# Decoder cross attention: two sequences per score group, both in two banks, one key folded out, and key and value jobs a whole bank wide

## The chip, the cores and the metric

The kernel runs on 1 core of one Trainium2 chip. The metric is the device time of one execution of the whole kernel in microseconds. The whole kernel is a chain of twelve blocks (attention, mixture of experts, recurrence and others) on one state x of 32 sequences x 32 tokens x 256 features; the change touches one block of them, the six-layer decoder.

## The reference, cut to what matters

Each of the 6 layers runs a masked self attention, a cross attention without a mask on 257 context keys, and a two-layer MLP, each followed by a residual sum and a layer norm. There are 16 heads of 16 features.

```
def mha(xq, xkv, W, B, mask):
    q = proj(xq, W[0], B[0]); k = proj(xkv, W[1], B[1]); v = proj(xkv, W[2], B[2])
    score = jnp.einsum('bhqd,bhkd->bhqk', q, k) / math.sqrt(DH)
    if mask is not None:
        score = jnp.where(mask[:, None] == 0, -10000.0, score)
    attn = jax.nn.softmax(score, axis=-1)
    ...
def step(x, p):
    h = mha(x, x, saw, sab, mask);   x = layer_norm(h + x, lg[0], lb[0])
    h = mha(x, enc, caw, cab, None); x = layer_norm(h + x, lg[1], lb[1])
    h = jax.nn.relu(x @ W1 + B1) @ W2 + B2; x = layer_norm(h + x, lg[2], lb[2])
```

## The kernel before, in words

All data are fp32. The 32 sequences are cut into NG = 8 tiles of GB = 4 sequences (4 x 32 tokens = 128 partitions). A position is one tile in one layer, 48 in all. `decoder_layers` is a software pipeline over 51 steps. At step s, self attention (part "sa") works on position s, the keys, values and queries of cross attention ("prep") on s-1, the cross attention itself ("ca") on s-2, and its output projection ("out") and the MLP ("dm") on s-3. Steps 3 to 47 hold all the parts.

A step has 8 units. Unit u of a step does the ca work of one of 2 feature halves (cc = u // 4) and one of 4 sequences (j = u % 4), and besides it the jobs that `UNIT_JOBS[u]` lists. A job is a group of matmuls into one of 4 ring banks, read out by VectorE ("dve") or ScalarE ("act"); each job waits until the job four before it has been read out (`RB = 4`). Jobs by name: K and V make keys and values of the context; n, q the queries; S0, S1q, S1k, S2, S3, S6, S7 are self attention (S3 scores, S2 values, S6 weights x values, S7 output projection); D0 to D3 the MLP; Y the output projection of cross attention; X the value of the last key, once a layer.

The ca work of a unit goes: `scores` (4 matmuls, each on 32 rows and 64 columns of the array, 257 keys, into banks 0 and 1), `maxima` on VectorE, two exponentials on ScalarE that also give the sums, then one unit later `transposes` (bank 2) and a copy to `pT` on ScalarE, and two units later `values` (bank 3). The 257th key (the first in memory) is not in `values`: its share is multiplied in later through `spread` and `last_v`. After the 4th sequence `reciprocals` and `own_heads` on VectorE turn sums and products into `attnT`.

Each engine runs its own list in program order, which is written out by hand: for TensorE

```
for it in range(N * U):
    if ca_unit(it):     scores(*ca_unit(it))
    if ca_unit(it - 1): transposes(*ca_unit(it - 1))
    for a in jobs_in(it): job(*a)
    if ca_unit(it - 2): values(*ca_unit(it - 2))
```

VectorE takes in each unit `maxima`, what was put off, the unit's jobs, then (by unit) `reciprocals`, `own_heads`, `own_queries` (unit 2), `self_shift` (unit 3: mask, row maximum, subtraction), `self_shares` (unit 4: sum, reciprocal, product and transpose into `sa_pT`), and last the second half of a layer norm. Job S6 waits for `sa_pT` and for the copy of S2's bank into `sa_v`.

## Time and profile before

| | us |
|---|---|
| median of 3 runs (lowest, highest) | 4612.44 (4609.56, 4612.98) |
| the profiled execution's own time | 4595.03 |
| its span from the first to the last instruction | 4593.2 |
| TensorE busy in the span | 4045.7 (88%) |
| VectorE busy | 2613.4 (57%) |
| ScalarE busy | 1853.6 (40%) |

The span is the time in which instructions run; busy times are sums over an engine's instructions. A busy share over the whole span mixes blocks with different limits; the decoder's ca units lie between about 774 and 2824 us of the span.

### The profile page before, as it was taken

What the parts mean: (1) busy time and instruction counts of PE and PEld (TensorE: products, weight loads), DVE (VectorE), ACT (ScalarE), POOL (GpSimd) and SP (SyncE); (2) the same over time, 40 slices, a digit from 0 to 9 for tenths busy, and PEclk for the clock granted to TensorE, in tenths of its full rate; (3) what the DMA queues carried; (4) which work ended last, traced back from release to release, by engine and by line L of the source; (5) the groups of instructions that cost most, each with busy time, mean ns of one, the idle gap of its engine ahead of it and who ended that gap; (6) DMA issues with size and microseconds to landing.
All of it is one profiled execution on the core that took longest, in us unless ns stands there. A gap on an engine that the chain in (4) does not pass through costs nothing. (4 is left out here: it accounts for less than half of the span.)

```text
span 4593.2 us, 105087 instructions
## 1 busy us (share of the span) xinstructions
PE 4045.7 (88%) x43842; PEld 3101.4 (68%) x43842; DVE 2613.4 (57%) x5580; ACT 1853.6 (40%) x5080; POOL 300.9 (7%) x560
## 2 busy tenths in 40 slices
PE   7988995999999999999999997779588787888867
PEld 6766884777777777777777775568345577566635
DVE  3435115777777777777777774721367654345545
ACT  1221221444444444444444443212266454255523
POOL 0000101000000000000000000010211000000000
PEclk9998997999999999999999998879799888888878
DMA  4110573011111111111111100048544300000000
GB/s 148 59 58 3 203 288 99 29 33 43 51 33 43 51 35 41 51 35 40 51 35 40 51 29 9 3 160 293 172 153 145 116 0 0 25 30 28 11 1 12
DMA packets 116921, 310.54 MB, mean 68 GB/s; under 512 B 29352, under 2 KB 75625, under 8 KB 92017
## 3 DMA queue, kind: packets, MB, share of 16 engines
q1 hardware_dynamic: 113392, 295.61, 18.8%
q0 software_dynamic: 3072, 8.39, 0.5%
q8 instruction: 342, 5.60, 0.5%
q14 instruction: 115, 0.93, 0.1%
HBM read 289.01 MB, written 14.94 MB: 66 GB/s over the span
## 5 line engine op out<-in xcount | busy, mean ns | idle before, releaser
L2490 ACT ACTIVATE layers_probs<-banks,layers_negmax 128x257 f32<-128x257 f32 x768 | 357.6, 471 | 1002.7 <-DVE layers_negmax L2369 1002.7
L2213 PE MATMUL banks<-ctx_tiles,weights_a 128*128 128x257 f32 x1536 | 397.4, 381 | 0.0
L2219 PE MATMUL banks<-weights_a,ctx_tiles 128*128 128x256 f32 x1536 | 379.4, 380 | 0.0
L2219 PEld LDWEIGHTS banks<-weights_a,ctx_tiles 128*128 128x128 f32 x1536 | 285.1, 191 | 35.4
L2369 DVE TENSOR_REDUCE layers_negmax<-banks 128x2 f32<-128x514 f32 x384 | 262.3, 683 | 71.5 <-PE banks L2274 71.5
L2213 PEld LDWEIGHTS banks<-ctx_tiles,weights_a 128*128 128x128 f32 x1536 | 270.9, 191 | 26.6 <-ACT layers_KT L2467 0.4
L2274 PE MATMUL banks<-layers_KT,layers_qblk 32*64 32x257 f32 x3072 | 256.2, 403 | 26.6 <-ACT layers_probs L2490 26.3
L2282 PEld LDWEIGHTS banks<-const,layers_probs 128*128 128x128 f32 x1536 | 162.2, 141 | 149.4 <-issue 149.3
L2282 PE MATMUL banks<-const,layers_probs 128*128 128x128 f32 x1536 | 253.6, 288 | 0.0
L2349 DVE TENSOR_TENSOR layers_V<-banks,rows_a 128x256 f32<-128x256 f32 x384 | 160.2, 418 | 138.8 <-PE banks L2219 132.9
L2495 ACT COPY layers_pT<-banks 128x512 f32<-128x512 f32 x384 | 223.5, 582 | 3.3 <-PE banks L2282 3.3
L2467 ACT ACTIVATE layers_KT<-banks,layers_ca_bk 128x257 f32<-128x257 f32 x384 | 184.2, 496 | 47.8 <-PE banks L2213 47.7
L2258 PE MATMUL banks<-layers_dm_nT,weights_b 128*128 128x128 f32 x1536 | 189.3, 277 | 0.6 <-ACT layers_dm_nT L2464 0.6
L2258 PEld LDWEIGHTS banks<-layers_dm_nT,weights_b 128*128 128x128 f32 x1536 | 184.8, 194 | 3.2 <-ACT layers_dm_nT L2464 0.9
L2263 PE MATMUL banks<-weights_b,layers_hid 128*128 128x256 f32 x768 | 173.8, 379 | 1.7 <-ACT layers_hid L2481 1.7
L2294 PEld LDWEIGHTS banks<-layers_pT,layers_V 128*32 128x32 f32 x6144 | 109.7, 109 | 87.8 <-issue 78.0
L2294 PE MATMUL banks<-layers_pT,layers_V 128*32 128x64 f32 x6144 | 163.6, 224 | 0.3 <-ACT layers_pT L2495 0.3
L2263 PEld LDWEIGHTS banks<-weights_b,layers_hid 128*128 128x128 f32 x768 | 145.7, 190 | 21.7 <-issue 2.1
L2490 ACT ACTIVATION_READ_ACCUMULATOR layers_probs<-banks,layers_negmax 128x1 f32 x768 | 150.6, 196 | 0.0
L2274 PEld LDWEIGHTS banks<-layers_KT,layers_qblk 32*64 32x64 f32 x3072 | 79.5, 130 | 96.4 <-issue 39.4
L2772 PE MATMUL banks<-weights_a,ctx_tiles 128*128 128x512 f32 x256 | 129.8, 636 | 1.0 <-DVE l2x_own L2847 0.5
L2345 DVE SCALAR_TENSOR_TENSOR weights_a<-banks,layers_sa_cols,const 128x1024 f32<-128x1024 f32 x96 | 118.4, 1274 | 7.3 <-PE banks L2206 7.3
(695 smaller groups left out, 8329.3 us busy)
## 6 DMA issues: line engine op xcount, KB each, us to landing
ctx_tiles<-in_ctx SPq DMA_DIRECT2D x65, 1028.0 KB, 5.1
weights_a<-in_L_w SPq DMA_DIRECT2D x44, 1024.0 KB, 5.4
l2x_B<-positions SPq DMA_DIRECT2D x32, 1280.0 KB, 5.9
weights_b<-in_L_w SPq DMA_DIRECT2D x32, 1024.0 KB, 6.2
weights_c<-in_L_w SPq DMA_DIRECT2D x16, 1024.0 KB, 7.1
weights_b<-in_L_xattn_w SPq DMA_DIRECT2D x12, 1024.0 KB, 7.4
l0x_key_rows<-in_ctx_rows SPq DMA_DIRECT2D x32, 256.0 KB, 2.7
ctx_tiles<-in_ctx_keys SPq DMA_DIRECT2D x32, 256.0 KB, 2.8
```

What stands on the lines that cost most here:

```text
L2213: last = mm(o[:, 0:LK], ca_wk[:, c, m * P:(m + 1) * P], E.ctx[:, tile % 2, c, j * LK:(j + 1) * LK], start=c == 0, stop=c == DC - 1)
L2219: last = mm(o[:, 0:D], E.ctx[:, tile % 2, c, first:first + P], ca_wv[:, c], start=c == 0, stop=c == DC - 1)
L2258: last = mm(o[:, i * P:(i + 1) * P], dm_w1[:, c, m * P:(m + 1) * P], dm_nT[:, c], start=c == 0, stop=c == DC - 1)
L2263: last = mm(o[:, 0:D], hid[:, m], dm_w2[:, m], start=m == 0, stop=m == FC - 1)
L2274: last = mm(ps[half, r // 2, 0:LK], qblk[rows, tile % 2, cc, j], KT[rows, tile % 2, cc, j * LK:(j + 1) * LK], start=True, stop=True)
L2282: last = tr(ps[:, TURN, (KC * t + c) * P:(KC * t + c + 1) * P], probs[:, cc, j, t, 1 + c * P:1 + (c + 1) * P], E.c("ident"))
L2294: last = mm(ps[32 * i:32 * (i + 1), PV, j * 64:(j + 1) * 64], V[:, pos % 2, KC * j + c, cc * P + 32 * i:cc * P + 32 * (i + 1)], pT[:, k % ...
L2349: last = v.tensor_tensor(V[:, tile % 2, arg], o[:, 0:D], E.rA[:, 0], ALU.add)
L2369: v.tensor_reduce(negmax[:, k % 2], ps[:, 0:2, 0:LK], AX.X, ALU.max, negate=True).then_inc(s["max_ready"], 1)
L2467: last = a(KT[:, pos % 2, m, j * LK:(j + 1) * LK], o[:, 0:LK], ACT.Identity, bias=ca_bk[:, m:m + 1])
L2490: a(probs[:, cc, j, t], ps[:, t, 0:LK], ACT.Exp, bias=negmax[:, k % 2, t:t + 1], accum_out=totals[:, cc, t, j:j + 1]).then_inc(s["exp_done ...
L2495: nc.scalar.copy(pT[:, k % 2].rearrange("p t c x -> p (t c x)"), ps[:, TURN]).then_inc(s["copied"], 1)
```

## The change

Two sequences (j and j+1) go together. In even units `scores` issues 8 matmuls for both, each 256 keys wide, and puts them side by side in banks 0 and 1; `maxima` is one reduction over 1024 elements for the pair and a small operation that takes the minimum of the negated maximum and 0; `exponentials` makes all four. `transposes` come two units after the scores instead of one, `values` of both sequences together at the end of each odd unit, and `pT` has 4 buffers instead of 2.

The last key is subtracted from the others: job XK (once a layer) projects it, ScalarE makes `less_last` = bias minus that key's value, and this is the bias with which K banks are read out. The last key's own score is then 0, its weight is exp(negmax), which ScalarE makes 8 at a time (`last_e`), and `reciprocals` adds it to the sums. A K job covers two sequences (512 columns), a V job both halves of one sequence, so a step has 4 of each instead of 8 of each, and they, S0 and S2 are moved among the units. S6 is no longer put off on VectorE, and the maxima come after what was put off. On ScalarE the copy of the transposes comes first, and in even units one job (two with XK) is read out before the exponentials.

```
     UNIT_JOBS = [
-        [k_job(0), v_job(0), k_job(1), v_job(1), ("S0", None, "act")],
-        [("S1q", None, "dve"), k_job(2), ("S1k", None, "act"), k_job(3), ("n", None, "act")],
-        [("q", None, "act"), k_job(4), ("Y", None, "dve"), ("S3", None, "dve")],
-        [k_job(5), v_job(2), k_job(6)],
-        [("D0", None, "act"), v_job(3), v_job(4), v_job(5)],
-        [("S2", None, "dve"), ("D1", 0, "act"), k_job(7), v_job(6), ("S6", None, "dve")],
-        [("D2", 1, "act"), v_job(7), ("X", None, "act")],
+        [("XK", None, "act"), ("S0", None, "act"), k_job(0), v_job(0)],
+        [("S1q", None, "dve"), k_job(1), ("S1k", None, "act"), ("n", None, "act")],
+        [("q", None, "act"), v_job(1), ("Y", None, "dve"), ("S3", None, "dve")],
+        [k_job(2), v_job(2)],
+        [("D0", None, "act"), k_job(3), ("S2", None, "dve")],
+        [("D1", 0, "act"), v_job(3), ("S6", None, "dve")],
+        [("D2", 1, "act"), ("X", None, "act")],
         [("S7", None, "dve"), ("D3", None, "dve")],
     ]
...
                     need(pe, "exp_done", 2 * k)
-                    for r in (0, 2, 1, 3):
-                        rows, half = slice(32 * r, 32 * (r + 1)), slice(64 * (r % 2), 64 * (r % 2 + 1))
-                        last = mm(ps[half, r // 2, 0:LK], qblk[rows, tile % 2, cc, j], KT[rows, tile % 2, cc, j * LK:(j + 1) * LK], start=True, stop=True)
+                    for a in range(2):
+                        for r in (0, 2, 1, 3):
+                            rows, half = slice(32 * r, 32 * (r + 1)), slice(64 * (r % 2), 64 * (r % 2 + 1))
+                            last = mm(ps[half, r // 2, a * KW:(a + 1) * KW], qblk[rows, tile % 2, cc, j + a], KT[rows, tile % 2, cc, (j + a) * KW:(j + a + 1) * KW], start=True, stop=True)
...
                 for it in range(N * U):
-                    if ca_unit(it):
+                    if it % 2 == 0 and ca_unit(it):
                         scores(*ca_unit(it))
-                    if ca_unit(it - 1):
-                        transposes(*ca_unit(it - 1))
+                    if ca_unit(it - 2):
+                        transposes(*ca_unit(it - 2))
                     for a in jobs_in(it):
                         job(*a)
-                    if ca_unit(it - 2):
-                        values(*ca_unit(it - 2))
+                    for back in (3, 2):
+                        if it % 2 and ca_unit(it - back):
+                            values(*ca_unit(it - back))
...
                 def maxima(k, pos, cc, j):
-                    dve.wait_ge(s["scores_done"], k + 1)
-                    v.tensor_reduce(negmax[:, k % 2], ps[:, 0:2, 0:LK], AX.X, ALU.max, negate=True).then_inc(s["max_ready"], 1)
+                    dve.wait_ge(s["scores_done"], k // 2 + 1)
+                    peak = negmax[:, cc, :, j:j + 2]
+                    link(v.tensor_reduce(peak, ps[:, 0:2].rearrange("p t (a x) -> p t a x", a=2), AX.X, ALU.max, negate=True))
+                    v.tensor_scalar(peak, peak, 0.0, None, ALU.min).then_inc(s["max_ready"], 1)
...
                 def reciprocals(k, pos, cc, j):
                     need(dve, "exp_done", 2 * (k + 1))
-                    link(v.reciprocal(rates[:, :, 0], totals[:, cc]))
-                    link(v.tensor_tensor(rates[:, :, 1], rates[:, :, 0], probs[:, cc, :, :, 0].rearrange("p j t -> p t j"), ALU.mult))
+                    dve.wait_ge(s["last_exp"], k // GB + 1)
+                    link(v.tensor_tensor(rates[:, :, 0], totals[:, cc], last_e[:, cc], ALU.add))
+                    link(v.reciprocal(rates[:, :, 0], rates[:, :, 0]))
+                    link(v.tensor_tensor(rates[:, :, 1], rates[:, :, 0], last_e[:, cc], ALU.mult))
...
-                    if ca_unit(it):
-                        maxima(*ca_unit(it))
                     for a in put_off:
                         take(*a)
                     put_off.clear()
+                    if it % 2 == 0 and ca_unit(it):
+                        maxima(*ca_unit(it))
                     for a in jobs_in(it):
-                        if a[3] in ("S3", "S6", "D3"):
+                        if a[3] in ("S3", "D3"):
...
                 def exponentials(k, pos, cc, j):
-                    act.wait_ge(s["max_ready"], k + 1)
-                    need(act, "transposed", k - U + 1)
+                    act.wait_ge(s["max_ready"], k // 2 + 1)
+                    need(act, "transposed", k + 1 - U + 1)
                     if j == 0:
                         need(act, "spread_ready", k // GB - 1)
-                    for t in range(2):
-                        a(probs[:, cc, j, t], ps[:, t, 0:LK], ACT.Exp, bias=negmax[:, k % 2, t:t + 1], accum_out=totals[:, cc, t, j:j + 1]).then_inc(s["exp_done"], 1)
+                    for i in (j, j + 1):
+                        for t in range(2):
+                            a(probs[:, cc, i, t], ps[:, t, i % 2 * KW:(i % 2 + 1) * KW], ACT.Exp, bias=negmax[:, cc, t, i:i + 1], accum_out=totals[:, cc, t, i:i + 1]).then_inc(s["exp_done"], 1)
+                    if j == GB - 2:
+                        a(last_e[:, cc], negmax[:, cc], ACT.Exp).then_inc(s["last_exp"], 1)
```

TensorE, units 4 and 5 of a full step before the change: `weights_c,layers_sa_nT` is S2, `layers_dm_nT` is D1, `layers_sa_pT,layers_sa_v` is S6.

```order
L2274 MATMUL banks<-layers_KT,layers_qblk 64x257 x4
L2282 MATMUL banks<-const,layers_probs 128x128 x4
L2199 MATMUL banks<-const,h_state 128x128 x2
L2219 MATMUL banks<-weights_a,ctx_tiles 128x256 x6
L2294 MATMUL banks<-layers_pT,layers_V 32x64 x8
L2274 MATMUL banks<-layers_KT,layers_qblk 64x257 x4
L2282 MATMUL banks<-const,layers_probs 128x128 x4
L2232 MATMUL banks<-weights_c,layers_sa_nT 128x256 x2
L2258 MATMUL banks<-layers_dm_nT,weights_b 128x128 x8
L2213 MATMUL banks<-ctx_tiles,weights_a 128x257 x2
L2219 MATMUL banks<-weights_a,ctx_tiles 128x256 x2
L2246 MATMUL banks<-layers_sa_pT,layers_sa_v 32x64 x32
```

The same units on TensorE after the change (L2284 scores, L2292 transposes, L2241 S2, L2267 D1, L2223 V, L2255 S6, L2304 values).

```order
L2284 MATMUL banks<-layers_KT,layers_qblk 64x256 x8
L2292 MATMUL banks<-const,layers_probs 128x128 x4
L2201 MATMUL banks<-const,h_state 128x128 x2
L2216 MATMUL banks<-ctx_tiles,weights_a 128x512 x2
L2241 MATMUL banks<-weights_c,layers_sa_nT 128x256 x2
L2292 MATMUL banks<-const,layers_probs 128x128 x4
L2267 MATMUL banks<-layers_dm_nT,weights_b 128x128 x8
L2223 MATMUL banks<-weights_a,ctx_tiles 128x256 x4
L2255 MATMUL banks<-layers_sa_pT,layers_sa_v 32x64 x32
L2304 MATMUL banks<-layers_pT,layers_V 32x64 x16
```

S2 has moved to the end of unit 4, ahead of unit 5's transposes; scores stand only in unit 4, values only at unit 5's end.

VectorE at the same place before the change, from the row maxima of self attention to the copy of S2's bank.

```order
L2404 TENSOR_REDUCE layers_sa_max<-layers_sa_sc 128x16
L2405 TENSOR_TENSOR layers_sa_sc<-layers_sa_sc,layers_sa_max 128x512
L2369 TENSOR_REDUCE layers_negmax<-banks 128x2
L2349 TENSOR_TENSOR layers_V<-banks,rows_a 128x256 x3
L2373 RECIPROCAL layers_rates<-layers_totals 128x2x4
L2374 TENSOR_TENSOR layers_rates<-layers_rates,layers_probs 128x2x4
L2375 TENSOR_TENSOR layers_spread<-const,layers_rates 128x512
L2409 TENSOR_REDUCE layers_sa_sum<-layers_sa_sc 128x16
L2410 RECIPROCAL layers_sa_sum<-layers_sa_sum 128x16
L2411 TENSOR_TENSOR layers_sa_sc<-layers_sa_sc,layers_sa_sum 128x512
L2412 STREAM_TRANSPOSE layers_sa_pT<-layers_sa_sc 128x512
```

And after the change, with the copy of S2's bank (L2362) among them.

```order
L2420 TENSOR_TENSOR layers_sa_sc<-layers_sa_sc,layers_sa_max 128x512
L2381 TENSOR_REDUCE layers_negmax<-banks 128x2x2
L2382 TENSOR_SCALAR layers_negmax<-layers_negmax 128x2x2
L2362 TENSOR_TENSOR layers_sa_v<-banks,const 128x1024
L2387 TENSOR_TENSOR layers_rates<-layers_totals,layers_last_e 128x2x4
L2388 RECIPROCAL layers_rates<-layers_rates 128x2x4
L2389 TENSOR_TENSOR layers_rates<-layers_rates,layers_last_e 128x2x4
L2390 TENSOR_TENSOR layers_spread<-const,layers_rates 128x512
L2424 TENSOR_REDUCE layers_sa_sum<-layers_sa_sc 128x16
L2425 RECIPROCAL layers_sa_sum<-layers_sa_sum 128x16
L2426 TENSOR_TENSOR layers_sa_sc<-layers_sa_sc,layers_sa_sum 128x512
L2427 STREAM_TRANSPOSE layers_sa_pT<-layers_sa_sc 128x512
```

The copy of S2's bank now stands ahead of the reciprocals and of the shares of self attention; before it came after them, behind one more reduction.

## Rows read from the trace of the kernel before

**Rows 1.** Windows of one step: busy us of each engine, clock, DMA.

```profile
1500.00:1543.00 43.00, 42.11 (x476) 32.40 (x475) 31.47 (x71) 19.79 (x64) 2.47 (x6) 1.00 0.31 107
```

**Rows 2.** Waits, 900 to 2700 us: engine, line, releaser: us, times, longest.

```profile
PEld banks L2199 <- DVE weights_a L2345: 38.3, 42, 0.9
```

**Rows 3.** TensorE timeline: start us, us, line, tiles [idle before <-releaser].

```profile
1502.25 0.66 PE L2274 MATMUL banks<-layers_KT,layers_qblk 32*64 32x257 f32 x8
1502.84 0.66 PE L2282 MATMUL banks<-const,layers_probs 128*128 128x128 f32 x4
1503.34 1.03 PE L2213 MATMUL banks<-ctx_tiles,weights_a 128*128 128x257 f32 x4
1504.20 1.03 PE L2219 MATMUL banks<-weights_a,ctx_tiles 128*128 128x256 f32 x4
...
1507.11 0.43 PE L2294 MATMUL banks<-layers_pT,layers_V 128*32 128x64 f32 x16
1507.47 0.66 PE L2274 MATMUL banks<-layers_KT,layers_qblk 32*64 32x257 f32 x8
...
1512.75 0.44 PE L2199 MATMUL banks<-const,h_state 128*128 128x128 f32 x2 [0.51 <-DVE weights_a L2345]
...
1517.71 1.07 PE L2238 MATMUL banks<-weights_a,layers_sa_k 128*32 128x256 f32 x16
1518.60 0.41 PE L2294 MATMUL banks<-layers_pT,layers_V 128*32 128x64 f32 x16
...
1523.53 0.66 PE L2274 MATMUL banks<-layers_KT,layers_qblk 32*64 32x257 f32 x8 [0.38 <-ACT layers_probs L2490]
...
1529.83 1.95 PE L2258 MATMUL banks<-layers_dm_nT,weights_b 128*128 128x128 f32 x16
1531.62 1.03 PE L2213 MATMUL banks<-ctx_tiles,weights_a 128*128 128x257 f32 x4
1532.49 1.03 PE L2219 MATMUL banks<-weights_a,ctx_tiles 128*128 128x256 f32 x4
1533.44 1.10 PE L2246 MATMUL banks<-layers_sa_pT,layers_sa_v 128*32 128x64 f32 x64
1534.36 0.41 PE L2294 MATMUL banks<-layers_pT,layers_V 128*32 128x64 f32 x16
1534.58 0.61 PE L2299 MATMUL banks<-layers_spread,const 128*32 128x256 f32 x8
```

**Rows 4.** VectorE timeline of the filling steps.

```profile
799.64 0.19 DVE L2373 RECIPROCAL layers_rates<-layers_totals 128x8 f32<-128x8 f32 x1
...
802.40 0.71 DVE L2412 STREAM_TRANSPOSE layers_sa_pT<-layers_sa_sc 128x512 f32<-128x512 f32 x1
...
803.62 1.21 DVE L2351 TENSOR_TENSOR layers_sa_v<-banks,const 128x1024 f32<-128x1024 f32 x1
```

**Rows 5.** VectorE timeline of a full step.

```profile
1523.28 0.77 DVE L2403 COPY_PREDICATED_SCALAR layers_sa_sc<-mask_zero,layers_floor 128x512 f32 x1
...
1525.41 0.69 DVE L2369 TENSOR_REDUCE layers_negmax<-banks 128x2 f32<-128x514 f32 x1
```

**Rows 6.** Groups by line, 900 to 2700 us: count, busy us, mean ns.

```profile
L2369 DVE TENSOR_REDUCE layers_negmax<-banks 128x2 f32<-128x514 f32 x335 | 228.7, 683 | 50.0 <-PE banks L2274 50.0
...
L2481 ACT ACTIVATE layers_hid<-banks,layers_dm_cols 128x128 f32<-128x128 f32 x332 | 96.3, 390 | 0.0
```

**Rows 7.** TensorE timeline of the filling steps.

```profile
780.19 0.44 PE L2199 MATMUL banks<-const,h_state 128*128 128x128 f32 x2 [1.75 <-ACT layers_KT L2467]
...
804.93 1.10 PE L2246 MATMUL banks<-layers_sa_pT,layers_sa_v 128*32 128x64 f32 x64 [1.53 <-DVE layers_sa_v L2351]
```

**Rows 8.** Windows of the filling steps, with the granted clock (PEclk).

```profile
781.00:784.00 3.00, 3.00 (x18) 2.65 (x14) 0.69 (x1) 1.54 (x6) 0.00 (x0) 0.50 0.00 0
...
800.00:805.00 5.00, 3.47 (x25) 2.69 (x25) 4.86 (x9) 1.27 (x5) 0.00 (x0) 1.00 0.00 0
```

**Rows 9.** TensorE timeline of the last steps.

```profile
2795.61 1.13 PE L2274 MATMUL banks<-layers_KT,layers_qblk 32*64 32x257 f32 x8 [2.81 <-ACT layers_probs L2490]
```

More of the change, by code:

```diff
@@ L2042, in decoder_layers @@
     VC = GB * KC
+    KW = KC * P
     U = DC * GB
@@ L2046, in k_job @@
     def k_job(i):
-        return ("K", (i // GB, i % GB), "act")
+        return ("K", (i // 2, i % 2), "act")
     def v_job(i):
@@ L2106, in decoder_layers @@
                     pos = parts[PART[kind]]
-                    if pos is not None and (kind != "X" or pos % NG == 0):
+                    if pos is not None and (kind not in ("X", "XK") or pos % NG == 0):
                         at[pos, kind, arg] = len(jobs)
@@ L2157, in _ @@
                         if step >= 2:
-                            need_job(sp, step - 2, "V", VC - 1)
+                            need_job(sp, step - 2, "V", GB - 1)
                         sp.dma_start(E.ctx[:, step % 2], A["ctx"][step % NG]).then_inc(s[f"ctx{step % 2}"], 16)
@@ L2171, in _ @@
                         send(layer, "w_ca_q")
-                        need_evacuated(sp, step - 1, "K", (DC - 1, GB - 1))
+                        need_evacuated(sp, step - 1, "K", (DC - 1, 1))
                         send(layer, "w_ca_k")
-                        need_evacuated(sp, step - 1, "V", VC - 1)
+                        need_evacuated(sp, step - 1, "V", GB - 1)
                         send(layer, "w_ca_v")
@@ L2212, in job @@
                         for c in range(DC):
-                            last = mm(o[:, 0:LK], ca_wk[:, c, m * P:(m + 1) * P], E.ctx[:, tile % 2, c, j * LK:(j + 1) * LK], start=c == 0, stop=c == DC - 1)
+                            keys = E.ctx[:, tile % 2, c].rearrange("p (j k) -> p j k", j=GB)[:, 2 * i:2 * i + 2, 1:LK]
+                            last = mm(o.rearrange("p (j k) -> p j k", j=2), ca_wk[:, c, m * P:(m + 1) * P], keys, start=c == 0, stop=c == DC - 1)
                     elif kind == "V":
-                        first = arg // KC * LK + 1 + arg % KC * P
                         if arg == 0:
                             need_weights(pe, "w_ca_v", pos)
-                        for c in range(DC):
-                            last = mm(o[:, 0:D], E.ctx[:, tile % 2, c, first:first + P], ca_wv[:, c], start=c == 0, stop=c == DC - 1)
+                        for b in range(KC):
+                            first = arg * LK + 1 + b * P
+                            for c in range(DC):
+                                last = mm(o[:, b * D:(b + 1) * D], E.ctx[:, tile % 2, c, first:first + P], ca_wv[:, c], start=c == 0, stop=c == DC - 1)
+                    elif kind == "XK":
+                        need_weights(pe, "w_ca_k", pos)
+                        for m in range(DC):
+                            for c in range(DC):
+                                last = mm(o[:, m * NB:(m + 1) * NB], ca_wk[:, c, m * P:(m + 1) * P], E.last[:, c], start=c == 0, stop=c == DC - 1)
                     elif kind == "X":
@@ L2290, in values @@
                         if cc == 0:
[L2291 removed]
+                            need_evacuated(pe, pos, "V", GB - 1)
                     for c in range(KC):
                         for i in range(4):
[L2294 removed]
+                            last = mm(ps[32 * i:32 * (i + 1), PV, j * 64:(j + 1) * 64], V[:, pos % 2, KC * j + c, cc * P + 32 * i:cc * P + 32 * (i + 1)], pT[:, k % 4, i // 2, c, 64 * (i % 2):64 * (i % 2 + 1)], start=c == 0, stop=c == KC - 1)
                     last.then_inc(s["pv_done"], 1)
@@ L2465, in take @@
                     elif kind == "K":
-                        m, j = arg
-                        last = a(KT[:, pos % 2, m, j * LK:(j + 1) * LK], o[:, 0:LK], ACT.Identity, bias=ca_bk[:, m:m + 1])
+                        m, i = arg
+                        for j in (2 * i, 2 * i + 1):
+                            seq = pos % NG * GB + j
+                            last = a(KT[:, pos % 2, m, j * KW:(j + 1) * KW], o[:, j % 2 * KW:(j % 2 + 1) * KW], ACT.Identity, bias=less_last[:, pos // NG % 2, m, seq:seq + 1])
+                    elif kind == "XK":
+                        for m in range(DC):
+                            a(last_k[:, m], o[:, m * NB:(m + 1) * NB], ACT.Identity, bias=ca_bk[:, m:m + 1]).then_inc(s["last_keys"], 1)
+                        act.wait_ge(s["last_keys"], DC * (pos // NG + 1))
+                        for m in range(DC):
+                            last = a(less_last[:, pos // NG % 2, m], last_k[:, m], ACT.Identity, scale=-1.0, bias=ca_bk[:, m:m + 1])
+                        last.then_inc(s["evac_act"], 1)
+                        need_evacuated(act, pos, "XK")
+                        return
                     elif kind == "q":
```

37 lines of the change are left out of this document (20 added, 17 removed).

## The prediction

> **What bounds the kernel now.** I first read the windows. In one 43 us stretch of the decoder TensorE is busy 42.11 us, VectorE 31.47, ScalarE 19.79, at full clock [rows 1]. Busy rows of matmuls overlap, so the share alone proves little; the waits say more. In 1800 us there is one TensorE wait of note that ends on VectorE, and it comes 42 times [rows 2]: a step lasts 1800 / 42 = 42.9 us, and there are 45 full steps. Then I read TensorE's timeline of a step [rows 3] by the distance from one group's start to the next group's start, since that, and not the duration, is what a group costs. Two places in a step show a wait: 0.51 us before job n at 1512.75 (its ring bank is the one of S1q, which VectorE reads out late; the weight loads waited 0.91 by [rows 2]) and 0.38 us before the scores at 1523.53 (exponentials of the unit before). Everything else is issue. So the decoder is bound by what TensorE issues; a saving there counts in full, and a new wait there counts in full too.
>
> **What the change takes off TensorE.** Prices by start-to-start [rows 3]: scores of one unit 0.59 (1502.25 to 1502.84), transposes 0.50, a K job 0.86, values 0.36 (1507.11 to 1507.47), but only 0.22 (1534.36 to 1534.58) where a group of the same shape of tiles stands on each side. A V job costs 0.95 (1532.49 to 1533.44) instead of some 0.86 where such a tiled group follows: entering costs about 0.1. Per pair of units before: twice (0.10 entry + 0.36 + 0.59 + 0.50) = 3.10 us. After, the pair has one entry 0.10, values 0.36 + 0.22, scores 0.59 plus a second set of four, transposes 0.50 once behind scores, and once behind an ordinary job, where I put 0.42 (an estimate: 0.50 less the cost of leaving the tiled scores, for which the 0.1 of entering is the nearest number).
>
> The trace of before has no second set of scores on the same rows of the array, so it is bounded. From below: pure streaming, one 257-column matmul, half a K job = 0.43, since the four run side by side. S3 shows two sets of four 256-column matmuls in 0.89 (1517.71 to 1518.60), which is 0.43 each and nothing over. From above: the whole 0.59 again. I take 0.43, as S3 is the nearest row. Then a pair costs 0.10 + 0.58 + 1.02 + 0.92 = 2.62, that is 0.48 less. One pair of the four stood behind S3, a tiled group already, and had no entry to lose: about 0.3. Sum: 3 x 0.48 + 0.3 = 1.74 us a step.
>
> The Trainium skill (TensorE: Matmul & The Clock Gate, Part 3, what overlaps and what doesn't) says that a weight load overlaps matmuls in flight only where the row group differs. The second set of scores uses the same four row groups again, so by that sentence its loads would wait for the first set and the second set would cost 0.59 or more, and the sum would lose 0.64 us a step. S3's two sets above speak against it, though S3 loads all 128 rows; no row here shows the case itself.
>
> K and V jobs: the same matmul columns in fewer, wider banks. K goes from 257 to 256 columns: 16 columns a step, 0.03 us. XK is four 32-column products once in eight steps: nothing. VectorE: 8 reductions of 683 ns [rows 6] become 4 over 1024 elements; a 1024-element operation took 1.21 [rows 4], so 4 x (1.21 + about 0.2 for the small one), 0.2 more in all; V reads lose 4 fixed parts, about 1 us less. ScalarE gets two small exponentials. All this lies under TensorE and costs nothing by itself; the cover is TensorE's 43 us against 31.5 and 20.
>
> **The old waits.** Job n's bank is now that of V0, read long before; S1q is now waited for by q (four jobs on), some 1.9 us later. Scores wait for exponentials issued two units back. Both waits go: the idle shown is 0.51 + 0.38 for matmuls and, with the weight loads' 0.91, more; I take 1.1.
>
> **The new wait.** S2 is moved to unit 4's end, and VectorE copies its bank before reciprocals and shares. From S2's last issue: 0.20 until the reader starts, copy 1.13 (start to next start, within the 1.21 of [rows 4]), reciprocals and shares of self attention in one go, 799.64 to 802.40 + 0.71 = 3.47 us for seven operations [rows 4], one added small operation 0.2, and 0.1 to TensorE: 5.1 us. TensorE meanwhile has transposes 0.42, D1 1.79 (1529.83 to 1531.62), V3 1.73 + 0.10 = 4.04 us before S6. So S6 waits 1.1 us in each step where before it did not. Behind it on TensorE stand values, shares and the next scores: all shift. Is VectorE free when S2 ends? V2 closes unit 3's jobs; from its last issue VectorE needs 0.2 + 0.6 (V2) + 2.13 (the self shift, 1523.28 to 1525.41 [rows 5]) + 1.4 (reduction) = 4.3 us, and TensorE needs values 0.68, scores 1.02, transposes 0.50, D0 0.21 (half of 0.42: two transposes), K 1.72, S2 0.86 = 5.0. There is 0.7 us to spare, plus the 0.2.
>
> D3 is a smaller one: D2's four reads take 4 x 0.39 less what they overlap, about 1.2 [rows 6], start 0.2 after D2, and TensorE has only transposes 0.42 to 0.50 and S7 0.87 in between (V7 stood there before). I charge 0.1.
>
> **The sum.** Per full step 1.74 + 0.03 + 1.1 - 1.1 - 0.1 = 1.7 us; 45 steps: 76 us. At the ends: the last two steps have no self attention, so no S6 wait, and now show waits of one round trip (scores, maxima, exponentials) per unit, up to 2.81 us [rows 9]; a trip per pair is fewer of them. I take 8 us there and -2 for the first steps, where D1 is missing and S6 waits longer. Total 82 us. The profiled execution took 4595.03 us with a span of 4593.2, 17 below the median 4612.44; its span would fall to about 4511, and the median by the same 82 to 4530.
>
> **Rivals.**
>
> A. The second sets overlap nothing: second scores 0.59, second values 0.36. A pair then saves 0.18 instead of 0.48, a step 0.6 + 1.1 - 1.2 = 0.5; 45 x 0.5 + 5 = 28: 4584. For it: the unknown is real. Against: S3. Chance 0.12.
>
> B. The gain is eaten by waits I have not seen. ScalarE now holds four exponentials (2 x 0.9 us) in front of K reads and copies that ring banks depend on, and VectorE a 1.4 us block. If such a wait takes 0.5 to 1 us a step: 4552 to 4575. For it: the margins above are 0.1 to 0.9 us. Chance 0.20.
>
> C. Slower: the S6 wait makes the clock fall. In the filling steps S6 once waited 1.53 us and the window around it kept the clock at 1.00, that is 2.4 GHz; after a wait of 1.75 us before job n the clock stood at 0.50, 1.2 GHz, for a 3 us window [rows 7, 8]: 3 us at half speed lose 1.5 us of work. It needs a wait 0.6 longer than mine, which VectorE gives if it reaches S2 late by more than its 0.9 of slack plus 0.6, for example if the 1024-element reduction runs at twice the time per element of [rows 6] and another read delays it. A step then gives 1.7 - 0.6 - 1.5 = -0.4, and the 8 us at the end hold: 4612 + 18 - 8 = 4622, up to 4650 if the fall lasts longer. It decides from a wait of about 1.7 us. Chance 0.08.
>
> D. Nothing: the savings on TensorE exist but waits in sum stay as large as 1.7 us more: 4603 to 4622. Chance 0.06.
>
> My own case, 4500 to 4550, has 0.54.
>
> **How the numbers follow.** The predicted time is my case's, 4530. Bounds: second scores as cheap as 0.35 and the wait at 0.9 with both old waits at their longer reading give 2.2 a step, 4505; the other side reaches through B and most of A to 4588. Outside lie C, D and the far end of A, 2 in 10 at most. The profile and the runs shown differ by 17 us, but the runs among themselves by 3.4; a difference of about 0.2% (9 us) can be told. Faster: my case, A, B, 0.85; within 0.2%: 0.06; slower: 0.09.
>
> **What would show it.** In the profile after: scores as one group of 16 rows with 1.0 us to the transposes (1.2 would be A); the two values groups 0.58 together; a TensorE wait before S6 (L2255) that ends on VectorE's transpose into sa_pT, about 1.1 us, once a step; no wait on weights_a (S1q) before job n, none on exponentials; steps of about 41.2 us; clock 1.00 throughout. A new releaser once a step elsewhere means B; a clock below 1.00 in the steady windows means C. The prediction is wrong if VectorE's order costs more than the one wait counted here.

## The result, and the profile after

| | before | after |
|---|---|---|
| median (lowest, highest) | 4611.0 (4605.97, 4612.98) | 4554.01 (4547.84, 4561.3) |
| span of the profiled execution | 4593.2 | 4547.8 |
| TensorE busy | 4045.7 | 3983.5 |

The ratio is 0.9879, 95% interval [0.9859, 0.9898]: 57 us off, where 82 were forecast (4530), inside the range of 4505 to 4588.

The windows view of the changed kernel for one step answers to [rows 1]. Columns: window, its length, busy us (and instructions) of TensorE, its weight loads, VectorE, ScalarE, GpSimd, then granted clock, DMA share, GB/s.

```profile
1505.79:1547.34 41.55, 40.48 (x463) 29.73 (x459) 31.53 (x69) 20.13 (x66) 2.48 (x6) 1.00 0.31 110
1200.00:2400.00 1200.00, 1167.78 (x13166) 858.86 (x13165) 904.56 (x1951) 582.48 (x1914) 71.74 (x174) 1.00 0.13 41
```

The step is 41.55 us long (1505.79 is a first scores group, 1547.34 the same group one step on) and TensorE is idle in 1.07 of them. The waits of 900 to 2700 us, as in [rows 2]:

```profile
PE banks L2255 <- DVE layers_sa_pT L2427: 45.6, 43, 1.2
```

The wait on `weights_a` that stood in [rows 2] has gone, and the one new entry of TensorE's that ends on VectorE is the S6 wait, 43 times, 45.6 us. Now TensorE's timeline of that step, which answers to [rows 3]:

```profile
1504.78 0.65 PE L2304 MATMUL banks<-layers_pT,layers_V 128*32 128x64 f32 x32
1505.25 0.61 PE L2309 MATMUL banks<-layers_spread,const 128*32 128x256 f32 x8
1505.79 1.09 PE L2284 MATMUL banks<-layers_KT,layers_qblk 32*64 32x256 f32 x16
1506.82 0.66 PE L2292 MATMUL banks<-const,layers_probs 128*128 128x128 f32 x4
...
1510.89 1.07 PE L2247 MATMUL banks<-weights_a,layers_sa_k 128*32 128x256 f32 x16
1511.89 0.66 PE L2292 MATMUL banks<-const,layers_probs 128*128 128x128 f32 x4
...
1515.92 0.66 PE L2304 MATMUL banks<-layers_pT,layers_V 128*32 128x64 f32 x32
1516.51 1.09 PE L2284 MATMUL banks<-layers_KT,layers_qblk 32*64 32x256 f32 x16
...
1520.82 0.60 PE L2292 MATMUL banks<-const,layers_probs 128*128 128x128 f32 x4
1521.26 1.95 PE L2267 MATMUL banks<-layers_dm_nT,weights_b 128*128 128x128 f32 x16
1523.05 1.89 PE L2223 MATMUL banks<-weights_a,ctx_tiles 128*128 128x256 f32 x8
1525.99 1.10 PE L2255 MATMUL banks<-layers_sa_pT,layers_sa_v 128*32 128x64 f32 x64 [1.05 <-DVE layers_sa_pT L2427]
...
1531.20 0.60 PE L2292 MATMUL banks<-const,layers_probs 128*128 128x128 f32 x4
1531.63 1.03 PE L2260 MATMUL banks<-weights_c,layers_sa_attnT 128*128 128x256 f32 x4
1532.68 1.53 PE L2272 MATMUL banks<-weights_b,layers_hid 128*128 128x256 f32 x6
```

Read from start to start: the scores of two sequences (x16 by the trace's count, x8 before; it counts each fp32 matmul of the program twice) 1.03 (1505.79 to 1506.82; one set was 0.59 before), values of two sequences 0.59, or 0.47 in front of the shares (1504.78 to 1505.25), transposes 0.49 behind scores and 0.44 behind an ordinary job (1520.82 to 1521.26). From V3 at 1523.05 to S6 at 1525.99 are 2.94 us: a V job is 1.73, the entry 0.10, so the wait is 1.11. S7 to D3 is 1.05 (1531.63 to 1532.68), where S7 took 0.87 before.

VectorE's timeline shows what S6 waits for:

```profile
1521.02 1.22 DVE L2362 TENSOR_TENSOR layers_sa_v<-banks,const 128x1024 f32<-128x1024 f32 x1 [0.83 <-PE banks L2241]
1522.16 0.16 DVE L2387 TENSOR_TENSOR layers_rates<-layers_totals,layers_last_e 128x8 f32<-128x8 f32 x1
...
1522.79 0.69 DVE L2390 TENSOR_TENSOR layers_spread<-const,layers_rates 128x512 f32<-128x512 f32 x1
1523.40 0.68 DVE L2424 TENSOR_REDUCE layers_sa_sum<-layers_sa_sc 128x16 f32<-128x512 f32 x1
...
1525.13 0.71 DVE L2427 STREAM_TRANSPOSE layers_sa_pT<-layers_sa_sc 128x512 f32<-128x512 f32 x1
```

VectorE had been idle for 0.83 us when S2's bank came. From there the copy, the reciprocals, the spread and the shares follow without a gap, to the end of the transpose at 1525.84: 4.82 us.

**Where the time went, step by step.** The 45 full steps (3 to 47) took 1937.08 us before and 1881.40 after: 55.7 off. They are not alike: 32 steps gained 1.39 (42.94 to 41.55), the five before a layer's first step 1.28, the five first steps of layers 0.77 (43.75 to 42.98), the first full one 0.35, and two gained 0.90 and lost 0.38. In that last one the profile shows 1.51 us of TensorE idle ahead of D2's matmuls, and gives no releaser; what it was stays open, but it isn't chance: the same two steps are longer in the run with another order of the scores, below (42.01 and 43.22 there, 42.04 and 43.32 here). The steps before and behind these 45 gained another 6.0 in sum, up to the decoder's last output projection. The decoder's 61.7 and the span's 45.4 differ mostly by blocks whose code did not change, which took longer in this one execution (9.1 us before the decoder, 7.7 behind it).

Job XK answers for the layer steps; TensorE's timeline in one:

```profile
1077.94 0.98 PE L2228 MATMUL banks<-last_keys,weights_a 128*128 128x32 f32 x8
1078.76 0.42 PE L2201 MATMUL banks<-const,h_state 128*128 128x128 f32 x2
```

Four products of only 32 columns (eight matmuls by the trace's count) hold TensorE for 0.82 us (1077.94 to 1078.76), once per layer. The trace of before had this price: job X has the same four products, and to the values behind it are 0.91, of which 0.10 is the entry into the tiled group:

```profile
1107.88 0.97 PE L2223 MATMUL banks<-last_keys,weights_a 128*128 128x32 f32 x8
1108.79 0.43 PE L2294 MATMUL banks<-layers_pT,layers_V 128*32 128x64 f32 x16
```

In the same steps X now stands behind D2 and covers D3's reads: S7 to D3 is 0.86 there (1114.41 to 1115.27). An ordinary step's 1.39 less 0.82, with D3's 0.26 back, gives 0.83; measured is 0.77.

### The profile page after: what moved, and what is told of

Read it like the earlier page. It is cut to its first block and busy times, and to the rows that moved or that the text cites. A ratio compares the mean times of both kernels' runs of the same rounds, so it can differ in the third digit from the quotient of the medians.

```text
span 4547.8 us, 103588 instructions
## 1 busy us (share of the span) xinstructions
PE 3983.5 (88%) x43122; PEld 2985.0 (66%) x43122; DVE 2617.2 (58%) x5484; ACT 1875.0 (41%) x5200; POOL 300.4 (7%) x560
## 5 line engine op out<-in xcount | busy, mean ns | idle before, releaser
L2223 PE MATMUL banks<-weights_a,ctx_tiles 128*128 128x256 f32 x1536 | 363.6, 380 | 0.0
L2216 PE MATMUL banks<-ctx_tiles,weights_a 128*128 128x512 f32 x768 | 363.2, 595 | 0.0
L2517 ACT ACTIVATE layers_probs<-banks,layers_negmax 128x256 f32<-128x256 f32 x768 | 354.2, 480 | 13.5 <-DVE layers_negmax L2382 6.5
L2223 PEld LDWEIGHTS banks<-weights_a,ctx_tiles 128*128 128x128 f32 x1536 | 285.2, 191 | 76.3 <-issue 46.5
L2360 DVE TENSOR_TENSOR layers_V<-banks,rows_a 128x512 f32<-128x512 f32 x192 | 130.8, 681 | 215.5 <-PE banks L2223 215.5
L2292 PE MATMUL banks<-const,layers_probs 128*128 128x128 f32 x1536 | 244.1, 281 | 3.4 <-ACT layers_pT L2524 2.8
L2292 PEld LDWEIGHTS banks<-const,layers_probs 128*128 128x128 f32 x1536 | 171.2, 141 | 107.1 <-issue 97.1
L2381 DVE TENSOR_REDUCE layers_negmax<-banks 128x4 f32<-128x1024 f32 x192 | 233.7, 1217 | 2.8 <-PE banks L2284 2.6
L2484 ACT ACTIVATE layers_KT<-banks,layers_less_last 128x256 f32<-128x256 f32 x384 | 162.1, 480 | 157.1 <-PE banks L2216 157.1
L2284 PE MATMUL banks<-layers_KT,layers_qblk 32*64 32x256 f32 x3072 | 211.3, 389 | 0.0
L2267 PE MATMUL banks<-layers_dm_nT,weights_b 128*128 128x128 f32 x1536 | 190.4, 278 | 3.8 <-issue 3.2
L2216 PEld LDWEIGHTS banks<-ctx_tiles,weights_a 128*128 128x128 f32 x768 | 131.7, 191 | 92.8 <-issue 92.7
L2267 PEld LDWEIGHTS banks<-layers_dm_nT,weights_b 128*128 128x128 f32 x1536 | 181.8, 194 | 4.5 <-issue 3.6
L2284 PEld LDWEIGHTS banks<-layers_KT,layers_qblk 32*64 32x64 f32 x3072 | 98.5, 132 | 74.0 <-issue 41.0
L2507 ACT ACTIVATE layers_hid<-banks,layers_dm_cols 128x128 f32<-128x128 f32 x384 | 110.5, 379 | 65.9 <-PE banks L2267 65.8
L2304 PE MATMUL banks<-layers_pT,layers_V 128*32 128x64 f32 x6144 | 127.2, 222 | 4.7 <-ACT layers_pT L2524 4.7
L2304 PEld LDWEIGHTS banks<-layers_pT,layers_V 128*32 128x32 f32 x6144 | 97.8, 110 | 45.5 <-issue 40.0
```

The source lines that it names most:

```text
L2216: last = mm(o.rearrange("p (j k) -> p j k", j=2), ca_wk[:, c, m * P:(m + 1) * P], keys, start=c == 0, stop=c == DC - 1)
L2223: last = mm(o[:, b * D:(b + 1) * D], E.ctx[:, tile % 2, c, first:first + P], ca_wv[:, c], start=c == 0, stop=c == DC - 1)
L2267: last = mm(o[:, i * P:(i + 1) * P], dm_w1[:, c, m * P:(m + 1) * P], dm_nT[:, c], start=c == 0, stop=c == DC - 1)
L2284: last = mm(ps[half, r // 2, a * KW:(a + 1) * KW], qblk[rows, tile % 2, cc, j + a], KT[rows, tile % 2, cc, (j + a) * KW:(j + a + 1) * KW], ...
L2292: last = tr(ps[:, TURN, (KC * t + c) * P:(KC * t + c + 1) * P], probs[:, cc, j, t, c * P:(c + 1) * P], E.c("ident"))
L2304: last = mm(ps[32 * i:32 * (i + 1), PV, j * 64:(j + 1) * 64], V[:, pos % 2, KC * j + c, cc * P + 32 * i:cc * P + 32 * (i + 1)], pT[:, k % ...
```

## The experiments

All edits are to the changed kernel ("after", 4554). Each ratio is to the kernel before, on the same chip. A step is the distance of two first scores groups.

**S2 ahead of K3.** The theory: S6 waits because the chain S2, copy, shares, transpose (5.1 us) is longer than what TensorE has behind S2. Then a K job of 1.72 between S2 and S6 must take the wait away. Rival: the chain hangs on something else than S2.

```
-        [("D0", None, "act"), k_job(3), ("S2", None, "dve")],
+        [("D0", None, "act"), ("S2", None, "dve"), k_job(3)],
```

> One swap in the changed kernel: job S2 goes ahead of K3 in unit 4. My theory (the 1.11 us wait of S6 is VectorE's chain from the read of S2's bank to the transposed weights): S2 is there 1.72 us earlier, VectorE is free of the pair's maxima 0.87 us earlier than it now starts on S2, so the S6 wait falls from 1.1 to 0.2 us and a full step from 41.55 to 40.7 us; the kernel some 39 us faster than the changed one, 4515. Rival (waits move rather than go, because VectorE and ScalarE are close to late at several places): another TensorE wait of 0.5 us or more a step appears and the step stays above 41.2.

Measured 4507.11 us, ratio 0.9773 [0.9757, 0.9789]; 40.62 us a step, 0.93 less. In the waits of 900 to 2700 us S6's 45.6 have shrunk to:

```profile
PE banks L2255 <- DVE layers_sa_pT L2427: 1.2, 5, 0.2
```

S6's wait hung on S2 and on what follows it. Some 0.2 of the 1.11 is left, as expected: V3 to S6 is 2.02 here (1507.83 to 1509.85), where V3 and the entry cost 1.83. One swap in a list is worth 0.0106 of the whole, 49 us, nearly as much as the change itself.

**S2 at the head of unit 5.** The K job stays in unit 4, the pair's transposes come ahead of S2.

```
-        [("D0", None, "act"), k_job(3), ("S2", None, "dve")],
-        [("D1", 0, "act"), v_job(3), ("S6", None, "dve")],
+        [("D0", None, "act"), k_job(3)],
+        [("S2", None, "dve"), ("D1", 0, "act"), v_job(3), ("S6", None, "dve")],
```

> The other way to undo the same wait: S2 goes back to the head of unit 5, where it stood before, so that VectorE does reciprocals and shares of self attention before it reads S2's bank. My theory: VectorE is through with the copy 4.75 us after it has the pair's maxima, TensorE reaches S6 at the same moment, the S6 wait falls to 0.2 us and now ends on the copy of S2 and not on the transpose; step 40.6 to 40.7 us, the kernel 4515. Rival (the wait is the price of S6 standing in unit 5 at all, whatever the order): no change, 41.5.

Measured 4509.86 us, ratio 0.9782 [0.976, 0.9804]; 40.64 a step and no wait at S6. The step is as expected, but TensorE has less behind S2 than in the changed kernel (1503.66 to 1508.13 is 4.47 us with S2's own 0.87, where it was 6.03 with the wait). VectorE's timeline tells why that is enough:

```profile
1503.17 0.17 DVE L2387 TENSOR_TENSOR layers_rates<-layers_totals,layers_last_e 128x8 f32<-128x8 f32 x1
...
1506.15 0.71 DVE L2427 STREAM_TRANSPOSE layers_sa_pT<-layers_sa_sc 128x512 f32<-128x512 f32 x1
1506.78 1.19 DVE L2362 TENSOR_TENSOR layers_sa_v<-banks,const 128x1024 f32<-128x1024 f32 x1
```

The reciprocals and shares now run ahead of S2's copy, since VectorE takes a unit's jobs before them and S2 isn't one of unit 4's any more. Behind S2 only the copy is left. So it was not only how late TensorE issued S2: the copy stood in front of 3.7 us of work (1522.16 to 1525.84), none of which needs S2, and S6 waits for the end of it. In the changed kernel VectorE sat idle for 0.83 us ahead of the copy with that work at hand; here the work begins right behind the maxima. TensorE's cover and VectorE's order are two cures of one wait, and either does it.

**S6 in unit 6.** S6 behind the scores and transposes of the next pair, ahead of D2.

```
-        [("D1", 0, "act"), v_job(3), ("S6", None, "dve")],
-        [("D2", 1, "act"), ("X", None, "act")],
+        [("D1", 0, "act"), v_job(3)],
+        [("S6", None, "dve"), ("D2", 1, "act"), ("X", None, "act")],
```

> S6 moves behind unit 6's transposes and ahead of D2, S2 stays. My theory: S6 no longer waits (TensorE reaches it at least 1.4 us after VectorE's transpose), one entry into tiled matmuls is added (0.1 us), and S7 is now waited for: VectorE reads S6 after own_heads and the maxima, about 0.4 us late; step 40.9 us, the kernel 4525. Rival: S7's wait takes the whole 1.1 and the step stays at 41.5.

Measured 4533.0 us, ratio 0.983 [0.9814, 0.9847]; 41.34 a step where 40.9 was expected. In TensorE's timeline the S6 wait is gone, but D3 now waits:

```profile
1524.45 1.03 PE L2260 MATMUL banks<-weights_c,layers_sa_attnT 128*128 128x256 f32 x4
1526.09 3.69 PE L2272 MATMUL banks<-weights_b,layers_hid 128*128 128x256 f32 x16 [0.61 <-DVE layers_y_sa L2331]
```

S7 at 1524.45 to D3 at 1526.09 is 1.64, 0.77 over S7's 0.87. ScalarE's timeline has D2's reads here:

```profile
1522.88 0.47 ACT L2517 ACTIVATE layers_probs<-banks,layers_negmax 128x256 f32<-128x256 f32 x1 [1.10 <-DVE layers_negmax L2382]
...
1524.79 1.15 ACT L2507 ACTIVATE layers_hid<-banks,layers_dm_cols 128x128 f32<-128x128 f32 x4
```

I had missed that: before the exponentials ScalarE reads out the unit's first job only, and that is now S6, a VectorE job. D2's reads stand behind four exponentials (1522.88 on) and end at 1525.94. VectorE's first read of S7's bank, which the profile names, ends then too (1525.93), so the view alone doesn't choose between the two. The kernel does: D3 waits for the reads of D1 and D2, both on ScalarE, and for the bank of the job four before it, which is V3's here, read out by 1520.01; it never waits for S7's read. The cause is ScalarE. The wait went from S6 to D3: an ordinary step gained 0.21 of the 1.11, and the whole kernel 0.0049, less than half of what the first swap gave.

**V3 out of S6's way.** This takes the cover away to make the wait about 2.8, and asks whether rival C's mechanism exists.

```
-        [("D1", 0, "act"), v_job(3), ("S6", None, "dve")],
-        [("D2", 1, "act"), ("X", None, "act")],
+        [("D1", 0, "act"), ("S6", None, "dve")],
+        [("D2", 1, "act"), v_job(3), ("X", None, "act")],
```

> The wait made longer: V3 moves from before S6 in unit 5 to behind D2 in unit 6, with nothing else changed. TensorE's work stays the same, S6's wait grows by V3's 1.73 us to 2.8, and D3's small wait (0.26 with the late first weights) goes. If the clock holds its 2.4 GHz level: step 41.55 + 1.73 - 0.26 = 43.0 us, 4620. The rival C of the prediction (such a wait makes the clock fall to 1.2 GHz): granted clock clearly below 1.00 in the steady windows, and 1.5 us more a step, 44.5 us, 4690.

Measured 4675.98 us, ratio 1.0143 [1.0124, 1.0162]: slower than before. Most steps took 44.3 to 44.9, few 43.0. First the wait in TensorE's timeline, then windows of 3 us behind two such waits, in neighbouring steps:

```profile
1527.18 1.10 PE L2255 MATMUL banks<-layers_sa_pT,layers_sa_v 128*32 128x64 f32 x64 [2.78 <-DVE layers_sa_pT L2427]
```

```profile
1570.00:1573.00 3.00, 2.80 (x104) 2.43 (x104) 1.19 (x5) 0.00 (x0) 0.00 (x0) 0.61 0.02 5
1573.00:1576.00 3.00, 3.00 (x35) 1.95 (x28) 2.50 (x7) 0.58 (x1) 0.00 (x0) 0.82 0.02 5
1527.00:1530.00 3.00, 2.82 (x120) 2.04 (x120) 1.63 (x6) 0.00 (x0) 0.00 (x0) 1.00 0.02 5
```

Both waits were 2.78 us. Behind the one at 1527.18 the clock stayed at 1.00 (2.4 GHz); behind the one that ended at 1570.20 it was 0.61 and then 0.82, a mean over both levels. Between 900 and 2700 us 30 of the 41 S6 groups took 1.4 us or more, where one takes 1.10 at full clock. So the wait of 1.7 us more a step costs 1.5 (the steps of 43.0, in which V3 also covers the D3 stage) to 3.3. The same wait doesn't always bring the fall: its length alone doesn't decide.

**The values of each unit apart.** One part of the change undone: the values two units behind their scores, singly, not two and two.

```
-                    for back in (3, 2):
-                        if it % 2 and ca_unit(it - back):
-                            values(*ca_unit(it - back))
+                    if ca_unit(it - 2):
+                        values(*ca_unit(it - 2))
```

> Of the pairing only the values are undone: each unit's values stand at the end of its own unit again, scores stay in pairs. My theory (a pair of values groups side by side costs 0.59, two apart cost 0.36 each and an entry of 0.1 more): TensorE issues 4 x 0.23 = 0.9 us more a step; 0.46 of it lies between S2 and S6 and shortens the S6 wait by as much; step 42.0 us, the kernel 4575. Rival (merged values save nothing, the whole gain is from scores): step at most 41.6.

Measured 4550.91 us, ratio 0.989 [0.987, 0.9909]; 41.63 a step; the whole can't be told from the changed kernel. In TensorE's timeline S6's wait is 0.54 instead of 1.05, and S7 to D3 is 0.86 with nothing of a wait:

```profile
1516.37 1.10 PE L2255 MATMUL banks<-layers_sa_pT,layers_sa_v 128*32 128x64 f32 x64 [0.54 <-DVE layers_sa_pT L2426]
...
1522.31 1.03 PE L2260 MATMUL banks<-weights_c,layers_sa_attnT 128*128 128x256 f32 x4
1523.17 3.62 PE L2272 MATMUL banks<-weights_b,layers_hid 128*128 128x256 f32 x16
```

The step lies far from my 42.0 and next to the rival's 41.6: I had counted what comes back at S6 and forgotten D3. The time alone would speak for the rival; the rows speak for an issue time that merging the values saves (0.09 net + 0.5 at S6 + 0.26 at D3 = 0.85) and that the waits eat: what is taken off in front of a wait makes it longer by as much. An experiment without waits, below, decides.

**Exponentials ahead of the unit's first job.** The change lets ScalarE read one job's bank before its four exponentials; this undoes it, and tests rival B's mechanism.

```
-                        while jobs_in(it)[early:early + 1] and early < 1 + (jobs_in(it)[0][3] == "XK"):
+                        while jobs_in(it)[early:early + 1] and early < 0:
```

> On ScalarE the four exponentials of a pair go before the unit's first job again, which puts the read of D2 behind them. My theory: D3 then waits 4 x 0.45 = 1.8 us more, D1 waits for D0's read about 1.0 but that only eats into the S6 wait; step 43.3 us, the kernel 4635; a TensorE wait on layers_hid once a step in the trace. Rival (the order on ScalarE does not matter, it is only 41% busy): step 41.5.

Measured 4672.53 us, ratio 1.0159 [1.0142, 1.0176]; 43.73 a step, many 45.4. TensorE's waits of 900 to 2700 us that end on ScalarE:

```profile
PE banks L2272 <- ACT layers_hid L2507: 68.5, 40, 1.9
...
PE banks L2267 <- ACT layers_dm_nT L2479: 40.3, 35, 1.2
```

Four exponentials in front of a bank's read cost TensorE 1.9 us at D3 and 1.2 at D1 in most steps; in the 43.73 us steps S6's wait is gone, as expected. The steps of 45.4 are 1.7 longer because the clock falls behind D3's wait: D3 takes 5.38 us there and 3.69 in the others.

```profile
1384.05 5.38 PE L2272 MATMUL banks<-weights_b,layers_hid 128*128 128x256 f32 x16 [1.94 <-ACT layers_hid L2507]
```

```profile
1384.00:1388.00 4.00, 3.95 (x11) 3.18 (x12) 1.26 (x3) 0.39 (x1) 0.60 (x2) 0.57 0.14 47
```

So rival C's mechanism shows here too, behind a wait of 1.94 in a full step, though not each time. By the ratios (1.0159 and 0.9879) this small part of the change is worth 129 us, more than the whole gain, the clock's falls included.

**V3 behind D2.** If the gain is issue less the waits, the order that leaves TensorE work behind both S2 and D2 must get all of it.

```
-        [("D0", None, "act"), k_job(3), ("S2", None, "dve")],
-        [("D1", 0, "act"), v_job(3), ("S6", None, "dve")],
-        [("D2", 1, "act"), ("X", None, "act")],
+        [("D0", None, "act"), ("S2", None, "dve"), k_job(3)],
+        [("D1", 0, "act")],
+        [("S6", None, "dve"), ("D2", 1, "act"), v_job(3), ("X", None, "act")],
```

> All waits taken away: S2 ahead of K3 in unit 4, only D1 in unit 5, unit 6 is S6, D2, V3. My theory: S6 comes 0.6 us after its weights are ready, S7 1.2 us after S6 has been read, D3 has V3's 1.73 us of cover; step 41.55 - 1.11 - 0.26 + 0.1 = 40.3 us, the kernel 4554 - 1.25 x 45 = 4498. Rival (TensorE's own issue costs the rest, or a wait appears where V3 is now read late): 40.9 or more.

Measured 4490.06 us, ratio 0.9759 [0.9738, 0.978]; 40.55 a step. The windows view has no idle TensorE:

```profile
1200.00:1500.00 300.00, 300.00 (x3415) 223.79 (x3414) 229.72 (x502) 151.23 (x498) 18.11 (x44) 1.00 0.15 48
```

S6 stands alone between transposes and D2 there, an entry and a leaving more than beside the values; with its group in its old place the step would be shorter.

**D2 in unit 5.** That is the next order.

```
-        [("D1", 0, "act"), v_job(3), ("S6", None, "dve")],
-        [("D2", 1, "act"), ("X", None, "act")],
+        [("D1", 0, "act"), ("D2", 1, "act"), ("S6", None, "dve")],
+        [v_job(3), ("X", None, "act")],
```

(with S2 ahead of K3, as above)

> Edit: the order of a step's stages in units 4, 5 and 6 becomes [D0, S2, K3], [D1, D2, S6], [V3, X]: the V job of the next step stands behind every stage of the self attention instead of between D2 and the last one. My theory (the gain is TensorE's saved issue time less the waits at S6 and D3, both of which come from what TensorE has in hand behind the stage before them): against the changed kernel's 41.55 us a step, the S6 wait of 1.1 us and the 0.26 us of the D3 stage go, and the extra change into row tiles and back that the version with S6 in unit 6 paid (about 0.2 us) goes too: 40.3 us a step, about 0.25 us below that version, some 10 us of the whole. Rival: S6 or D3 waits again, because D1 and D2 stand side by side and S6's values follow them too soon: 40.6 us a step or more, a wait of its own listed at the values or at D3.

Measured 4498.35 us, ratio 0.9755 [0.9739, 0.9771]; 40.31 a step, 0.24 below the last, as expected. In TensorE's timeline S6 (1504.89) follows D1 and D2 at once, and D3 (1511.35) follows S7 0.87 later:

```profile
1501.08 3.74 PE L2267 MATMUL banks<-layers_dm_nT,weights_b 128*128 128x128 f32 x32
1504.89 1.10 PE L2255 MATMUL banks<-layers_sa_pT,layers_sa_v 128*32 128x64 f32 x64
...
1510.48 1.03 PE L2260 MATMUL banks<-weights_c,layers_sa_attnT 128*128 128x256 f32 x4
1511.35 3.62 PE L2272 MATMUL banks<-weights_b,layers_hid 128*128 128x256 f32 x16
```

The whole kernel did not follow: the two ratios can't be told apart. In the profiled executions the decoder, from its first matmul to the first of the next block, did: 2006.4 us here, 2014.9 there, 8.5 less. Step 2, the first with scores, gave 3.4 back (36.93 against 33.49), since S6 waits 3.86 us there with no MLP jobs yet to cover it; and the blocks before the decoder, whose code is the same, took 16 us longer in this execution.

**Values apart, where nothing waits.** The merging once more: the edit of "The values of each unit apart", now in the order just shown.

> Edit: in the order [D0, S2, K3], [D1, D2, S6], [V3, X], in which no TensorE wait is left in a full step (40.31 us), the values of each unit are again issued two units later by themselves instead of two and two. My theory: there the issue time that merging them saves is no longer eaten by a wait. In the changed kernel the same edit cost 0.09 us a step and gave back 0.5 at S6 and 0.26 at D3, 0.85 of issue in all; here nothing is there to give back, so the step grows by 0.8 to 41.1 us, and the kernel by 0.8 x 46 = 37 us, to about 4535. Rival: the merging is worth only the 0.09 us that it showed there (the waits were shorter for another reason): 40.4 us and 4502.

Measured 4515.93 us, ratio 0.9821 [0.98, 0.9843]; 41.03 a step: 0.72 more than with merged values, 0.0066 of the whole, 30 us. The same edit that made no difference clear of noise in the changed kernel is worth 30 us here, so the rival (0.09) is out. The 0.13 that lacks to 0.85 is a last wait at S6 that I had overlooked in the order with merged values. From D1 to S6 are 3.81 there (1501.08 to 1504.89) and 3.67 here, in TensorE's timeline:

```profile
1494.88 3.74 PE L2267 MATMUL banks<-layers_dm_nT,weights_b 128*128 128x128 f32 x32
1498.55 1.10 PE L2255 MATMUL banks<-layers_sa_pT,layers_sa_v 128*32 128x64 f32 x64
```

And with merged values VectorE had S6's weights ready only at 1504.74, 0.15 before S6:

```profile
1504.03 0.71 DVE L2427 STREAM_TRANSPOSE layers_sa_pT<-layers_sa_sc 128x512 f32<-128x512 f32 x1
```

So 0.14 of the saving was still eaten, and 0.72 + 0.14 = 0.86.

**Order within a scores group.** Which matmuls may stand side by side?

```
-                    for a in range(2):
-                        for r in (0, 2, 1, 3):
+                    for r in (0, 2, 1, 3):
+                        for a in range(2):
```

> Edit: the sixteen score matmuls of a unit are issued with the row group as the outer loop and the two banks as the inner one, so that two matmuls of one row group stand back to back instead of four row groups in turn. Nothing else differs from the changed kernel. My theory: the 1.03 us of a scores group holds only because neighbours lie on different rows of the array; on the same rows the second waits for the first, the four groups no longer run side by side, and a group takes about 2.1 us: +1.1 us in each of four units, 4.4 us a step, 46 us a step and about 4750 us. Rival: the order within the group does not matter, because the weights of the second are loaded while the first runs: 41.5 us a step, 4554 us.

The inner loop of the edit is over the pair's two sequences, the two halves of one bank, and not over the two banks, as the expectation has it; the program issues eight matmuls, which the trace counts as sixteen.

Measured 4553.74 us, ratio 0.9877 [0.9861, 0.9894], 41.62 a step. The theory fell; in TensorE's timeline the group costs 1.04 from start to start instead of 1.03:

```profile
1506.29 1.11 PE L2284 MATMUL banks<-layers_KT,layers_qblk 32*64 32x256 f32 x16
1507.33 0.66 PE L2292 MATMUL banks<-const,layers_probs 128*128 128x128 f32 x4
```

## Why the prediction was right, and where it was short

**The bound** held: TensorE's issue sets the step; every run above moves by what TensorE's list gains, less what it waits.

**Second sets on the same rows** were put at 0.43 and 0.22. Measured 1.03 - 0.59 = 0.44 for scores (S3's 0.89 is not two times 0.43 with nothing over, but with 0.03). For values the pair is 0.59, or 0.58 as predicted. Rival A is out. By the Trainium skill (TensorE: Matmul & The Clock Gate, Part 3, what overlaps and what doesn't) a weight load overlaps matmuls in flight only where the row group differs. By that sentence the prediction put the second set at 0.59 or more; the measured 0.44, and the 1.04 of the group with the same row group back to back, both speak against it here.

**The issue saving** was put at 1.74 and came out at 1.61: three ordinary pairs went from 3.10 to 2.64 (entry 0.10, values 0.59, scores 1.02, transposes 0.49 and 0.44), and the fourth saved 0.23 instead of 0.3, because transposes behind S3 took 1.00 from S3's start (1510.89 to 1511.89) where a tiled group took 0.89: leaving such a group costs about 0.1 too, which I had charged only to the transposes behind scores.

**The old waits** (put at 1.1) are gone; by start distances they were 1.14. **The S6 wait** was put at 1.1 and is 1.11 by start distances; taking it away gave 0.93 and 0.91, with some 0.2 left on TensorE in either. Its size was right and its chain too, with the copy of S2's bank at its head; that the copy stood there by VectorE's order and not by need, the working did not see.

**D3** was put at 0.1 and costs 0.26: 0.18 between S7 and D3 and 0.08 in D3 itself (3.62 instead of 3.54 to the next group). The term is mis-sized: D2's four reads on ScalarE run from 1531.40 to 1532.54 and D3 starts 0.14 later; from D2's last issue (1531.20) that is 1.48, and TensorE has 1.30 in between. The working had left out the 0.14 from the end of the reads to D3's start, which it had counted, as 0.1, at S6. With the values apart D3 comes 0.36 later, and waits for nothing.

So an ordinary step gains 1.61 + 1.14 - 1.11 - 0.26 = 1.38 (measured 1.39) and not 1.7. 32 such steps make 10 of the 21 us by which the 45 x 1.7 = 76.5 fell short to 55.7.

**XK as "nothing"** was wrong, though job X showed its price in the trace of before: 0.82 us in each of five steps, which gained 0.77; against 1.7 that is 4.7 us, with 2.0 in the steps before them. The rest is the first full step (1.3) and the two odd ones (2.9). **The ends** were put at 6 and gave 6.0, which is luck: -2 and 8 were forecast, and the two misses of 1.3 cancel. The first steps lost 3.3, where S6 waited 2.19 us and the clock stood at 0.50 afterwards, and the last gained 9.3. TensorE's timeline and two windows of the first steps:

```profile
782.21 1.50 PE L2255 MATMUL banks<-layers_sa_pT,layers_sa_v 128*32 128x64 f32 x64 [2.19 <-DVE layers_sa_pT L2427]
```

```profile
781.00:785.00 4.00, 2.79 (x71) 2.65 (x71) 2.82 (x7) 0.00 (x0) 0.00 (x0) 0.72 0.74 267
785.00:789.00 4.00, 4.00 (x23) 2.31 (x22) 1.57 (x5) 0.47 (x2) 0.00 (x0) 0.50 0.00 0
```

**Rivals.** B's time (4552 to 4575) is where the result fell, but not by its reason: no new wait beside S6 and D3 came, since the early read on ScalarE keeps the four exponentials out of the way, as undoing it showed. C's mechanism is real: it showed in full steps behind waits of 2.78 us and of 1.94, though not behind each. The full steps of the changed kernel, with a wait of 1.05, never came to it (clock 1.00 from 1200 to 2400).

## What to carry to other kernels

Price a saving on the bounding engine by the next wait behind it in its list: the same merge was worth 0.09 us a step in front of two waits and 0.72 where next to nothing waited. When a change thins out the list between a stage and the one that needs its result, look for an order that fills both gaps before measuring the merge: here that gave another 0.012 of the whole, as much as the change itself. A small job isn't free because its columns are few: four products of 32 columns cost 0.82 us.
